# The quantised feed-forward with its batches overlapped and one multiply on GpSimd, and the router's scatter on a queue of its own

## What is computed

```python
def fp4_quant_dequant(x):
    xb = x.reshape(shape[:-1] + (shape[-1] // 16, 16))
    scale = jnp.maximum(jnp.max(jnp.abs(xb), axis=-1, keepdims=True) / 6.0, 1e-12)
    xn = xb / scale
    q = _GRID[jnp.searchsorted(_MID, jnp.abs(xn))] * jnp.sign(xn) * scale
    return q.reshape(shape)
gate = fp4_linear(x, w_gate)      # x and the weight both quantised; 128 -> 352
y = fp4_linear(x, w_up)           # 128 -> 352
h = jax.nn.silu(gate) * y
return fp4_linear(h, w_down)      # h quantised too; 352 -> 128
```

## Time and profile before

| | us |
|---|---|
| median of 3 runs | 4421.69 |
| lowest and highest | 4418.83, 4434.67 |
| the profiled execution | 4445.3 |
| its span | 4443.5 |

### The profile page before, as it was taken

One profiled execution on the slowest core, in us unless ns is written; L12 is line 12 of the kernel. 1 busy time (PEld: TensorE's weight loads), 2 busy tenths in 40 slices (PEclk: granted clock), 3 DMA queues, 4 the chain that ended last, 5 costly groups with the idle time before them and its releaser, 6 DMA issues. The chain is left out here.

```text
span 4443.5 us, 68068 instructions
## 1 busy us (share of the span) xinstructions
PE 2959.2 (67%) x21547; PEld 1611.6 (36%) x21547; DVE 2377.8 (54%) x4808; ACT 1767.3 (40%) x4259; POOL 809.7 (18%) x1093
## 2 busy tenths in 40 slices
PE   5588734285443678777887577877777630768885
PEld 2344323154332344444444333333333320752221
DVE  4566466454674566666664344445544441137775
ACT  2355412121111455545554244444444300227675
POOL 2100000021001444444442300000000007022220
PEclk9789866587665899999998666666666655879998
DMA  3422110000001000000000477777777514663331
GB/s 112 76 53 50 40 43 0 8 1 6 0 0 43 19 15 18 18 18 17 10 18 9 140 189 188 189 194 194 189 190 197 135 41 142 169 133 53 58 56 38
DMA packets 457690, 340.63 MB, mean 77 GB/s; under 512 B 64351, under 2 KB 418842, under 8 KB 457378
## 3 DMA queue, kind: packets, MB, share of 16 engines
q1 hardware_dynamic: 434562, 302.49, 27.9%
q0 software_dynamic: 11008, 27.28, 2.1%
q10 hardware_dynamic: 11808, 7.08, 0.6%
HBM read 174.71 MB, written 146.81 MB: 72 GB/s over the span
## 5 line engine op out<-in xcount | busy, mean ns | idle before, releaser
L1156 DVE TENSOR_REDUCE a_soft_NM<-a_soft_s_ps 128x2 f32<-128x1024 f32 (+3 forms) x512 | 515.2, 1021 | 235.3 <-PE a_soft_s_ps L1091 133.3
L1190 ACT ACTIVATE a_soft_PTS<-a_soft_st_ps 128x512 f32<-128x512 f32 (+3 forms) x1024 | 458.9, 523 | 173.5 <-PE a_soft_st_ps L1067 101.9
L465 PE MATMUL a_soft_pt_ps<-net_ident,a_soft_PR 128*128 128x128 f32 x1280 | 328.2, 369 | 116.1 <-ACT a_soft_PTS L567 110.4
L613 ACT ACTIVATE a_soft_PR<-a_soft_s_ps,a_soft_least 128x128 f32<-128x128 f32 (+3 forms) x512 | 263.6, 526 | 341.3 <-DVE a_soft_least L588 227.1
L1062 PE MATMUL a_soft_st_ps<-a_soft_QS,a_soft_KS 50*128 50x512 bf16 (+4 forms) x1024 | 263.0, 365 | 72.8 <-ACT a_soft_PTS L1190 40.7
L465 PEld LDWEIGHTS a_soft_pt_ps<-net_ident,a_soft_PR 128*128 128x128 f32 x1280 | 182.7, 180 | 214.7 <-ACT a_soft_PR L613 154.6
L1104 PE MATMUL a_soft_o_ps<-a_soft_PTS,a_soft_VR 128*32 128x512 f32 (+3 forms) x2048 | 249.5, 562 | 0.1
L2212 PE MATMUL f_run_ps<-f_run_WQKV,f_run_HT 128*128 128x512 f32 x384 | 229.5, 689 | 15.5 <-DVE f_run_RS L1433 8.3
L2545 ACT ACTIVATE f_run_PB<-f_run_ps,f_run_MX 128x128 f32<-128x128 f32 x512 | 179.8, 377 | 136.6 <-DVE f_run_MX L2427 136.6
L2350 POOL TENSOR_TENSOR f_run_QK<-f_run_QK,f_run_T 128x512 f32<-128x512 f32 x128 | 163.2, 1275 | 366.4 <-DVE f_run_T L2405 363.9
L569 DVE COPY a_soft_PTS<-a_soft_pt_ps 128x512 f32<-128x512 f32 (+3 forms) x320 | 169.4, 529 | 69.3 <-PE a_soft_pt_ps L465 42.2
(11 more groups left out here) (376 smaller groups left out, 6473.5 us busy)
## 6 DMA issues: line engine op xcount, KB each, us to landing
a_soft_BIAS<-skew_d SPq DMA_DIRECT2D x256, 191.0 KB, 4.2
band_d<-a_soft_PR SPq DMA_DIRECT2D x256, 191.0 KB, 3.7
skew_d<-a_soft_RS SPq DMA_DIRECT2D x128, 256.0 KB, 4.4
a_soft_PB<-band_d SPq DMA_DIRECT2D x128, 256.0 KB, 3.1
f_run_W<-in_L_ffn_w SPq DMA_DIRECT2D x72, 256.0 KB, 2.7
a_soft_QS<-query_rows_d SPq DMA_DIRECT2D x32, 384.0 KB
query_rows_d<-a_proj_PARTS SPq DMA_DIRECT2D x72, 128.0 KB
query_rows_d<-a_proj_PARTS POOLq DMA_DIRECT2D x72, 128.0 KB
```

What stands on the lines that cost most here:

```text
L465: last = pe.transpose(pt_ps[:, slot, kb * P:(kb + 1) * P], PR[:, n % NPR, OFF + kb * P:OFF + (kb + 1) * P], ident[:])
L613: act.activation(PR[:, n % NPR, OFF:OFF + width(j)], s_ps[:, n % 4, 0:width(j)], ACT.Exp, bias=least[:, n:n + 1], scale=-1.0).then_inc(pro ...
L1156: dve.tensor_reduce(NM[:, T % 2, j, p, :], s_ps[:, ring["s", a] % 2, :, 0:width(j)], AX.X, ALU.max, negate=True).then_inc(max_ready, 1)
L1190: act.activation(PTS[:, T % 2, 2 * p + par, kb, q0:S], st_ps[:, e % 3, q0:S], ACT.Exp, scale=scale).then_inc(probs_ready, 1)
```

## The change

In **fp4_ffn** the loops over batches become straight code in another order, with the following parts.

- HH, sc and t have two buffers each. The quantisation of x has scratch of its own (scx, invx, tx, mx).
- fp4 can be called with q None: it then stops after the subtract (L1258), nine instructions.
- POOL does what the tenth did for h: it waits for `h_rounded` and multiplies t by the block scales into HH, 128x1408, once a batch, and signals `hq_ready`. For x the tenth instruction stays on DVE.
- DVE, in batch b: multiply tiles 0 and 1; quantise x of batch b + 1; multiply tiles 2 and 3; nine instructions on h of batch b; add y of batch b - 1.
- PE, in batch b: gate and up of tiles 2 and 3; turn h of batch b - 1; turn x of batch b + 1; down product of batch b - 1; gate and up of tiles 0 and 1 of batch b + 1. ACT follows this order.

In **split_projection**, where there is a scatter (a3_proj alone), SP issues all 12 stores of a projection, and POOL issues the 64 indirect DMAs at once with no wait for the projections. The other two projections (a0_proj, a2_proj) issue what they did.

```diff
                 for dst, table in jobs[i % NJ][3]:
-                    for row, p in table[0::2]:
-                        sp.dma_start(dst[...], PARTS[:, i % 4, p, :]).then_inc(stored[i % 4], 16)
+                    for n, (row, p) in enumerate(table):
+                        if n % 2 == 0 or spread is not None:
+                            sp.dma_start(dst[...], PARTS[:, i % 4, p, :]
+                                         ).then_inc(stored[i % 4] if n % 2 == 0 else stored_too[i % 4], 16)
...
         @block.gpsimd
         def _(pool):
+            if spread is not None:
+                rows, slots, to = spread
+                for t in range(NT):
+                    for k in range(2):
+                        pool.indirect_dma_start(to[:, :], bass.IndirectOffsetOnAxis(slots[:, k, t:t + 1], 0), rows[:, t, :], None
+                                                ).then_inc(scattered, 16)
+                pool.wait_ge(scattered, 16 * 2 * NT)
+                return
...
-                if spread is not None:
-                    rows, slots, to = spread
-                    for t in range(i * NT // N, (i + 1) * NT // N):
...
-    dve.tensor_tensor(t, t, m, ALU.subtract)
+    last = dve.tensor_tensor(t, t, m, ALU.subtract)
+    if q is None:
+        return last
     dve.drain()
     return dve.tensor_tensor(blocks(q), blocks(t), bcast(sc, FP4_BLOCK), ALU.mult)
...
+        @block.gpsimd
+        def _(pool):
+            if clear is not None:
+                pool.memset(zeros[:], 0.0).then_inc(zeroed, 1)
+            for b in range(B):
+                pool.wait_ge(h_rounded, b + 1)
+                pool.tensor_tensor(HH[:, b % 2, :].rearrange("p (b k) -> p b k", k=FP4_BLOCK), t[:, b % 2, :].rearrange("p (b k) -> p b k", k=FP4_BLOCK),
+                                   bcast(sc[:, b % 2, :], FP4_BLOCK), ALU.mult).then_inc(hq_ready, 1)
...
+            for b in range(B):
+                multiply(b, 0)
+                multiply(b, 1)
+                if b + 1 < B:
+                    round_x(b + 1)
+                multiply(b, 2)
+                multiply(b, 3)
                 dve.drain()
+                if b >= 2:
+                    dve.wait_ge(hq_ready, b - 1)
+                fp4(dve, HH[:, b % 2, :], None, sc[:, b % 2, :], inv[:], t[:, b % 2, :], m[:]).then_inc(h_rounded, 1)
                 dve.drain()
+                if b >= 1:
+                    add(b - 1)
+            add(B - 1)
...
+            def turn_h(b):
                 pe.wait_ge(hq_ready, b + 1)
...
+            turn_x(0)
+            gate_up(0, 0)
+            gate_up(0, 1)
+            for b in range(B):
+                gate_up(b, 2)
+                gate_up(b, 3)
+                if b >= 1:
+                    turn_h(b - 1)
+                if b + 1 < B:
+                    turn_x(b + 1)
+                if b >= 1:
+                    down(b - 1)
+                if b + 1 < B:
+                    gate_up(b + 1, 0)
+                    gate_up(b + 1, 1)
+            turn_h(B - 1)
+            down(B - 1)
```

More of the change, by code:

```diff
@@ L1348, in batch, with multiply, add @@
[L1348 to L1351, removed]
+            def multiply(b, j):
+                dve.wait_ge(silu_ready, TB * b + j + 1)
+                dve.tensor_tensor(HH[:, b % 2, j * FF:(j + 1) * FF], G[:, j % 2, :], u_ps[:, j % 2, 0:FF], ALU.mult).then_inc(h_made, 1)
+            def add(b):
+                dve.wait_ge(y_ready, b + 1)
+                xs = X[:, TB * b:TB * b + TB, :].rearrange("p a f -> p (a f)")
+                dve.tensor_tensor(xs, y_ps[:], xs, ALU.add).then_inc(y_added, 1)
@@ L1367, in _, with turn_x @@
+            add(B - 1)
         @block.tensor
         def _(pe):
-            with pe.Fori(0, B) as b:
+            def turn_x(b):
                 pe.wait_ge(xq_ready, b + 1)
+                if b >= 1:
+                    pe.wait_ge(xqt_ready, b)
                 for j in range(TB):
@@ L1393, in _, with copy_x, silu, copy_h @@
                 last.then_inc(y_ready, 1)
+            turn_x(0)
[4 more added lines that the diff above has]
+                gate_up(b, 3)
+                if b >= 1:
+                    turn_h(b - 1)
+                if b + 1 < B:
+                    turn_x(b + 1)
+                if b >= 1:
+                    down(b - 1)
[4 more added lines that the diff above has]
+            down(B - 1)
         @block.scalar
         def _(act):
-            with act.Fori(0, B) as b:
+            def copy_x(b):
                 act.wait_ge(xt_ready, b + 1)
                 act.activation(XQT[:], xt_ps[:], ACT.Copy).then_inc(xqt_ready, 1)
[L1400 to L1404, removed]
+            def silu(b, j):
+                act.wait_ge(gu_ready, TB * b + j + 1)
+                if TB * b + j >= 2:
+                    act.wait_ge(h_made, TB * b + j - 1)
+                act.activation(G[:, j % 2, :], g_ps[:, j % 2, 0:FF], ACT.Silu).then_inc(silu_ready, 1)
+            def copy_h(b):
                 for c, (c0, n) in enumerate(CH):
                     act.wait_ge(ht_ready, 3 * b + c + 1)
-                    act.activation(HQT[0:n, c, :], ht_ps[0:n, c % 2, :], ACT.Copy).then_inc(hqt_ready, 1)
+                    if c == 0 and b >= 1:
+                        act.wait_ge(y_ready, b)
+                    act.activation(HQT[0:n, c, :], ht_ps[0:n, (3 * b + c) % 2, :], ACT.Copy).then_inc(hqt_ready, 1)
+            copy_x(0)
+            silu(0, 0)
+            silu(0, 1)
+            for b in range(B):
+                silu(b, 2)
+                silu(b, 3)
+                if b >= 1:
+                    copy_h(b - 1)
+                if b + 1 < B:
+                    copy_x(b + 1)
+                    silu(b + 1, 0)
+                    silu(b + 1, 1)
+            copy_h(B - 1)
 TWO_PI = (6.28125, 0.001935005187988281, float(2 * np.pi - 6.28125 - 0.001935005187988281))
```

44 lines of the change are left out of this document (22 added, 22 removed).

## The result

| | before | after |
|---|---|---|
| median, us | 4422.7 (4 runs, 4418.8 to 4434.7) | 4271.3 (4 runs, 4260.7 to 4280.4) |
| profiled execution, us | 4445.3 | 4260.7 |
| f0_run, first instruction to end of the last add | 228.4 | 169.7 |
| f1_run, the same | 229.9 | 172.2 |
| a3_proj, first instruction to the next stage's first | 125.3 | 89.5 |

The ratio is 0.9654, 95% interval 0.9635 to 0.9673. The change is faster by 151 us; 137 were forecast, and 4271 lies in the range of 4263 to 4328. The three stages give 58.6 + 57.7 + 35.8 = 152.1 us, which is all of the difference of the medians.

The account below looks back on a forecast made before the run. Feed-forwards were taken as bound by one chain through DVE and PE, a3_proj by POOL's DMA issues; savings of 107 + 30 = 137 us from 4421.7 gave 4285, range 4263 to 4328.

Parts of the forecast that it names:

- batch 7: Feed-forward's last batch, no x behind it: DVE waits for gate and up of tiles 2 and 3, 15.5 us.
- tail: End of a feed-forward: POOL's multiply 3.0 us, then turn, down and add as before, 9.1: 12.1 us.
- The round: Feed-forward, batches 2 to 6: DVE's work 19.05 us, plus 0.2 waiting for POOL and 0.3 for code.
- a joint of 0.08: Feed-forward, DVE's round: 0.08 us added to each term of DVE's work.
- The code term: Feed-forward: 0.3 us a batch allowed for code that is no longer a loop, between 0 and 1.
- The hold: Feed-forward: POOL's multiply blocks DVE's instructions on SBUF alone, not those with PSUM input; DVE waits 0.2 us a batch.
- POOL's multiply: Feed-forward: h's 128x1408 multiply by block scales on POOL takes 2.9 us, between 2.5 and 3.5.
- rivals 2 and 4: Feed-forwards, POOL's multiply costs more by block: 2, 4 to 7 us, chance 0.09; 4, slower than before, chance 0.02.
- Rival 1: Feed-forwards: PE becomes the bound, at its lower clock throughout; 40 us less saved, 4325; chance 0.10.
- The allowance of 1.3: a3_proj: indirect DMAs that meet DVE's instructions cost up to 2.4 us, so 30 us was taken instead of 31.3.
- the 11.4 us from the last issue's end to the next stage: End of a3_proj: the time from POOL's last issue to the next stage stays at 11.4 us.
- rival 3: a3_proj: SP's stores end last, after POOL's indirect DMAs; 4298 to 4315 us; chance 0.10.

Follow-up runs that it names:

- e6: Changed kernel with x's multiply by its scales on POOL too, two buffers for x's rounded values and scales: 4252.0 us, ratio 0.9637.
- e1: Changed kernel with h's multiply by its scales back on DVE, overlap kept: ratio 0.9685 to the kernel before.
- e4: Changed kernel with a second POOL multiply of the same size behind each first, on tiles nothing else reads: ratio 0.9694 to the kernel before.
- e3: Kernel before, loops and order kept, with h's multiply on POOL and scratch of its own for x: ratio 1.0056.
- e9: Changed kernel with x's multiply on POOL too, run again beside the changed kernel on one chip: 4244.2 us, ratio 0.9624.
- e7: Changed kernel with the down product made twice into the same PSUM tile: ratio 0.9658 to the kernel before.
- e2: Kernel before with the change of split_projection alone: ratio 0.9907, a3_proj 89.8 us.
- e5: Kernel before with SP issuing all stores in a3_proj, POOL still waiting for each projection before its 8 indirect DMAs: ratio 0.9929, a3_proj 95.1 us.

## Why the prediction was right

It was right in direction and, for the feed-forwards, in mechanism; 151 us came where 137 were forecast. In a3_proj one step was wrong, and in f0_run's last batch another. Its terms, against the changed kernel:

| f0_run, us | forecast | measured |
|---|---|---|
| start to the first h rounded | 30.4 | 30.2 |
| batch 1 | 19.5 | 18.95 |
| batches 2 to 6 | 97.8 | 93.4 |
| batch 7 | 15.5 | 17.35 |
| tail | 12.1 | 9.9 |
| sum | 175.3 | 169.7 |

**The round was 19.55, and is 18.6.** Three small terms were too large. I gave every instruction a joint of 0.08, also where no drain stands and the next begins before the one ahead has ended: a pair of multiplies takes 0.94 or 0.95 instead of 1.20, and the multiplies start 0.61 behind the add (623.81 to 624.42), not 0.77. That is 0.67 of the 0.95. The code term, 0.3 a batch, is a gap in one round of three that costs 0.35 there. The hold was right, 0.2, by luck: POOL was 0.3 us quicker, DVE came to its first locked instruction 0.5 sooner, and that instruction ends 0.04 us after POOL (626.38 to 626.42), where I let it begin only then. In batch 1 the wait was to be 0.95; L1246 took 0.99 there, 0.81 more than alone.

**POOL's multiply** was put at 2.9 us from the row of its own kind, between 2.5 and 3.5; it is 2.59. Scaling 1.04 us for 512 elements by elements scales the fixed part with them. There is no cost by block: that was rivals 2 and 4, and both are refuted by every one of the 16 rows. In e6 512 elements with a scale for every 16 take 1.06 us, with one for every 64 they took 1.04. The Trainium skill (GPSIMD Engine Reference, section 3.1) has some 2.6 cycles an element at 1.2 GHz for two inputs, by which 1408 elements would be an estimated 3.05 us; the rows have 1.84 ns an element, 2.2 cycles, and here the rows decide.

**The hold.** "Right: one DVE instruction on x's scales lengthened in batches 1 to 7": it is L1246, and e1 and e4 show its cause from both sides, gone with POOL's multiply, while beside a second one an instruction of the same kind is held for 1.9 us. What the rows ahead of the prediction could not show is shown: a TENSOR_SCALAR with one input in SBUF is held. On 128x512 this kind takes 0.43 us, a TENSOR_TENSOR 0.69, so it is a faster form. The reduce and the reciprocal beside POOL's multiply are not held, nor are the multiplies and the add with an input in PSUM. The rule of the Trainium skill (SBUF — State Buffer, "SBUF: two separate sides") is an exclusive lock held for the whole instruction, which DVE takes in its 2-port performance modes and with two SBUF inputs; the 2.04 us of e4 agree. It was no argument against the change, since POOL's multiply was put where DVE has 2.3 us of work that needs no lock. In e3 one reduce is all that stands between, and L1244 takes 1.65 us instead of 0.18. That costs nothing there, as DVE later waits for y all the same (40.5 us in eight waits); what e3 loses is PE's wait for h.

**Batch 7 and PE.** Here the step was wrong. Gate and up of the last two tiles were to take 1.2 us each and be done with 5.1 us after batch 6; it was 7.3. PE had stood idle for 5.4 us before them, and they ran at the lower level of its clock. These stretches of the changed kernel, columns as in the earlier trace rows, are those two tiles in batch 7, a down product with the next gate and up in a middle round, the last product of f0_run, and the first two us of the last product of f1_run:

```profile
718.30:723.10 4.80, 4.77 (x8) 2.76 (x9) 0.93 (x2) 0.46 (x1) 1.44 (x1) 0.51 0.00 0
...
632.90:638.00 5.10, 5.09 (x32) 4.11 (x32) 4.67 (x6) 0.91 (x2) 0.00 (x0) 1.00 0.01 3
...
740.70:743.70 3.00, 2.94 (x24) 2.75 (x24) 0.00 (x1) 0.00 (x0) 0.00 (x0) 1.00 0.00 0
...
1220.60:1222.60 2.00, 1.96 (x9) 1.96 (x10) 0.00 (x0) 0.00 (x0) 0.00 (x0) 0.50 0.00 0
```

At the granted clock of 0.51, the lower level, gate and up of two tiles take 4.8 us, twice the forecast; behind a down product, at 1.00, two tiles and the product together take 5.3 (632.91 to 638.23). The last product takes 2.94 us at the upper level (f0_run) and 4.90 where it begins at the lower (f1_run), against 4.73 in the forecast: that is 1.8 of the 2.2 us by which the tail of f0_run came out shorter, and POOL's multiply most of the rest. f1_run's tail is 11.8. The 4.73 was one of sixteen products of the kernel before, which take 2.94 to 5.49, and the short tail is luck: in e1, e4 and e9 the last product of f0_run takes 5.49, 5.49 and 5.46. For the rounds it changes nothing, as e7 shows: the silu that DVE wants is 5.5 us early (637.54 against 643.02), where the forecast had some 4. Rival 1 is refuted at this load.

**a3_proj** was to give 30, and gave 35.8. POOL took 81.3 us for its 64 against 82.3, and started 0.4 later than I let it. The allowance of 1.3 for indirect DMAs that meet DVE's instructions wasn't needed on top: two of them take 1.24 and 1.10 us beside DVE's L783, but all such time in the 64 is 0.7 us, and the 81.3 hold it. The rest, 3.9 us, is the step that failed: that the 11.4 us from the last issue's end to the next stage stay. They don't: it is 7.5 us in the changed kernel, in e2 and in e5. The prediction held them fixed, whatever POOL had issued before. The landing of the last indirect DMA is fixed, 1.3 us. But the most of the rest is GpSimd's drain, and that changed with what POOL had issued: 9.20 us in before and e3, with 112 DMAs, and 5.27 in the changed kernel and the eight other runs, with 64, 0.08 us for each DMA in both. e5 leaves the order and the waits of the indirect DMAs as they were and only takes the stores off POOL, and the drain goes with them. What GpSimd does in the drain no run shows, and it is no plain count everywhere: at the end of a0_proj, behind 48 stores alone, it takes 5.6 to 6.4 us. SP was ready 14 us before POOL at 0.65 us a store, where I had 0.75; rival 3 is refuted.

## What to carry to other kernels

Two engines that wait for each other in turn are worth a new order before anything is made faster: here the overlap gave 97.8 us in two stages and the moved multiply 18.5, and in the old order that same move lost 22.5. An instruction moved to GpSimd costs DVE little (0.2 us a batch here) if it starts where DVE's next two microseconds read PSUM or reduce; list DVE's instructions from that point up to the first TENSOR_SCALAR or the first with two SBUF inputs, and compare their sum with POOL's duration. Stores issued by GpSimd in a stage that it ends cost their issue time and, in this stage, 0.08 us each in GpSimd's drain ahead of the barrier.

## What the runs showed that I had not expected

- A DVE instruction of 0.18 us on one input of 32 values took 2.04 beside POOL's multiply (e4), while a reciprocal and a reduce beside it kept their 0.35 and 0.68.
- A multiply on GpSimd with scales per 16 elements takes 2.59 us for 1408, and 1.06 for 512 (e6): 1.5 us for 896 more elements, 1.7 ns each, and some 0.2 us fixed.
- In the changed kernel DVE's straight code has a gap of 0.43 us in one round of three.
- GpSimd's drain at the end of a3_proj takes 9.20 us behind 112 DMAs and 5.27 behind 64, while no DMA moves and no other engine works.
- The same last product of a stage takes 2.94 us in one run and 5.49 in another, by PE's granted clock: a difference of some 2 us between two stages is no reading of the change.
